# Attention 1 of a two-layer decoder: probabilities normalised on GpSimd, mask added on two blocks of three

## The reference, cut to what matters

```
x = x + L0_attn(layernorm(x)); x = x + L0_ssm(ctx, layernorm(x)); x = x + L0_ffn(layernorm(x))
x = x + L1_attn(layernorm(x)); x = x + L1_ssm(ctx, layernorm(x)); x = x + L1_moe(layernorm(x))

# L1_attn: B=4 (batches of x), S=256, H=16 query heads, 4 key/value heads, D=128
q, k = layernorm(q) * g + b, layernorm(k) * g + b          # then rotary embedding
scores  = q @ k^T / sqrt(D)                                 # 256 x 256 for each (batch, head)
scores  = where(causal, -inf, scores)
weights = softmax(scores)                                   # exp(s - max) / sum
attn    = weights @ v
out     = concat(attn over heads) @ w_o^T
```

## Time and profile before

| what | us |
|---|---|
| median of 3 runs (lowest, highest) | 913.45 (911.21, 914.03) |
| the profiled execution | 913.75 |
| its span, from the first to the last instruction | 912.0 |
| TensorE busy, over the span | 767.7 (84%) |
| VectorE busy | 703.3 (77%) |
| ScalarE busy | 445.6 (49%) |
| GpSimd busy | 340.6 (37%) |
| chain that ended last: TensorE, VectorE, issue, ScalarE, GpSimd | 50%, 26%, 11%, 9%, 3% |

### The profile page before, as it was taken

How to read it: one execution, slowest core, us unless ns; L and a number is a source line. 1 busy time by engine, 2 the same in 40 slices (tenths; PEclk the granted TensorE clock), 3 DMA queues, 4 the chain that set the end, 5 groups by cost and what they waited for, 6 DMA issues and landing times.

```text
span 912.0 us, 12288 instructions
## 1 busy us (share of the span) xinstructions
PE 767.7 (84%) x3984; PEld 563.1 (62%) x3984; DVE 703.3 (77%) x1229; ACT 445.6 (49%) x928; POOL 340.6 (37%) x242
## 2 busy tenths in 40 slices
PE   6771459877798996799999999999955799999997
PEld 2241346554433563477767776777743689999996
DVE  4869779889857976999999999999977544444443
ACT  1663368650336402666566556756642354444442
POOL 1001346552330422233333323432343286666663
PEclk9785579998799998999999999999987899999999
DMA  4313223345020212011111211111300243334431
GB/s 171 121 47 114 93 94 125 115 139 218 1 98 0 74 43 92 19 40 44 51 36 36 69 36 36 55 39 36 118 0 1 79 158 138 138 138 138 141 135 46
DMA packets 28884, 74.63 MB, mean 82 GB/s; under 512 B 3633, under 2 KB 6337, under 8 KB 28449
## 3 DMA queue, kind: packets, MB, share of 16 engines
q1 hardware_dynamic: 28384, 71.51, 23.2%
q10 hardware_dynamic: 448, 2.49, 0.8%
HBM read 72.55 MB, written 1.44 MB: 81 GB/s over the span
## 4 chain that ended last, share of the span: by engine, by line
PE 50%; DVE 26%; issue 11%; ACT 9%; POOL 3%; DMA 1%; POOLq 0%; DVEq 0%; SPq 0%; ACTq 0%
PE ps L1671 6%; PE ps L1785 6%; PE ps L1786 6%; PE ps L1787 6%; PE ps L1631 4%; DVE hS L976 3%; PE ps L1651 3%; PE ps L1750 3%; PE ps L1435 2%; PE ps L1738 2%; DVE arena L1280 2%; DVE hS L1006 2%; DVE ps L968 2%; PE ps L1408 1%; PE ps L1720 1%
## 5 line engine op out<-in xcount | busy, mean ns | idle before, releaser
L403 POOL TENSOR_TENSOR hS<-hS,BCb 128x512 f32<-128x512 f32 x64 | 81.6, 1278 | 131.9 <-issue 66.7
L1387 DVE SCALAR_TENSOR_TENSOR arena<-ps,arena 128x1024 f32<-128x1024 f32 x32 | 39.2, 1224 | 102.2 <-ACT arena L842 93.1
L426 POOL TENSOR_TENSOR hS<-hS,BCb 128x1024 f32<-128x1024 f32 x23 | 56.1, 2440 | 111.3 <-DVE ps L968 96.3
L1671 PE MATMUL ps<-WB,hT 128*128 128x512 f32 x192 | 88.0, 603 | 3.0 <-DVE arena L1261 2.0
L476 POOL TENSOR_TENSOR MHl<-arena,MHh 128x1024 fp32r<-128x1024 f32 x34 | 81.7, 2404 | 16.9 <-ACT MHh L845 16.9
L1416 PE MATMUL ps<-ident,hS 128*128 128x128 f32 x256 | 40.1, 311 | 54.7 <-POOL hS L426 31.2
L1785 PE MATMUL ps<-Wh,MHh 128*128 128x256 f32 x272 | 77.8, 286 | 6.0 <-POOL MHl L476 6.0
L1006 DVE TENSOR_TENSOR_SCAN hS<-dA,ps 128x512 f32<-128x512 f32 x64 | 78.1, 1220 | 2.2
L1786 PE MATMUL ps<-Wl,MHh 128*128 128x256 f32 x272 | 77.6, 285 | 0.0
L1787 PE MATMUL ps<-Wh,MHl 128*128 128x256 f32 x272 | 77.5, 285 | 0.0
L1416 PEld LDWEIGHTS ps<-ident,hS 128*128 128x128 f32 x256 | 32.6, 159 | 65.1 <-POOL hS L426 38.2
(11 more groups left out here) (233 smaller groups left out, 1967.4 us busy)
## 6 DMA issues: line engine op xcount, KB each, us to landing
BCb<-bc_dram SPq DMA_DIRECT2D x32, 512.0 KB, 3.7
BCb<-bcq_dram SPq DMA_DIRECT2D x64, 256.0 KB, 3.1
arena<-gate_dram SPq DMA_DIRECT2D x32, 512.0 KB, 3.7
WB<-in_we SPq DMA_DIRECT2D x34, 256.0 KB, 2.7
WB<-in_wqkv SPq DMA_DIRECT2D x1, 3072.0 KB, 12.7
WA<-in_wo ACTq DMA_DIRECT2D x1, 2048.0 KB, 7.7
WA<-in_ffn SPq DMA_DIRECT2D x1, 1408.0 KB, 7.9
pkb<-in_pk SPq DMA_DIRECT2D x2, 698.0 KB, 4.7
```

The source lines that it names most:

```text
L403: gp.tensor_tensor(h, h, qbc(q)[:, 1:2, :].broadcast_to([P, DT, S]), ALU.mult).then_inc(s["c_ready"], 1)
L426: gp.tensor_tensor(h, h, BCb[g % SB_LOADS][:, 1:2, :].broadcast_to([P, DT, HALF]), ALU.mult).then_inc(s["c_ready"], 1)
L1671: last = mm(ps[:, bank + t, :], hT[:, c, P * (2 * b + t):P * (2 * b + t) + P], WB[:, c, c0:c0 + 512], start=(c == 0), stop=(c == HC - 1))
```

## The change

Two edits, both in attention 1.

The two multiplications by the reciprocal move from VectorE to GpSimd. VectorE keeps the reciprocal, under the entry "norm" of the plan, and GpSimd takes the same entry for the multiplications. The reciprocal of unit u now also waits until GpSimd has finished unit u - 2, whose reciprocals lie in the same buffer; TensorE's transposes wait for the same semaphore as before, which GpSimd now raises.

The mask matmul writes and reads blocks 0 and 2 of the three only, 256 columns for 384. The middle block is not written by it any more; L1720's second half is the first to write there.

```diff
@@ GpSimd
+            def norm1(u):
+                p = u % 2
+                pool.wait_ge(s["s1_rc"], u + 1)
+                gp.tensor_scalar(P1[p][:, 0:P], P1[p][:, 0:P], rc1[:, p, 0:1], None, ALU.mult).then_inc(s["s1_norm"], 1)
+                gp.tensor_scalar(P1[p][:, P:3 * P], P1[p][:, P:3 * P], rc1[:, p, 1:2], None, ALU.mult).then_inc(s["s1_norm"], 1)
+
             for kind, a in ATT1_PLAN:
                 if kind == "sum":
                     job(JOB[a])
+                elif kind == "norm":
+                    norm1(a)
                 elif kind == "dbu" and a > Q_IN_FFN:
                     times_cq(a - 1)
@@ VectorE
-            def norm1(u):
+            def rc1_calc(u):
                 p = u % 2
                 dve.wait_ge(s["s1_exp"], 2 * (u + 1))
+                if u >= 2:
+                    dve.wait_ge(s["s1_norm"], 2 * (u - 1))
                 v.reciprocal(rc1[:, p, :], sum1[:, p, :]).then_inc(s["s1_rc"], 1)
-                dve.wait_ge(s["s1_rc"], u + 1)
-                v.tensor_scalar(P1[p][:, 0:P], P1[p][:, 0:P], rc1[:, p, 0:1], None, ALU.mult).then_inc(s["s1_norm"], 1)
-                v.tensor_scalar(P1[p][:, P:3 * P], P1[p][:, P:3 * P], rc1[:, p, 1:2], None, ALU.mult).then_inc(s["s1_norm"], 1)
...
                 elif kind == "norm":
-                    norm1(a)
+                    rc1_calc(a)
@@ TensorE
-                mm(ps[:, 2 + p, 0:3 * P], identb[:], mask1[:], start=True, stop=True, skip_group_check=True)
+                diagonal = lambda z: z.rearrange("p (k n) -> p k n", k=3)[:, 0::2, :]
+                mm(diagonal(ps[:, 2 + p, 0:3 * P]), identb[:], diagonal(mask1[:]), start=True, stop=True, skip_group_check=True)
```

## The result

The kernel after the change has a median of 922.12 us (921.12 to 922.98); the kernel before, measured beside it, 913.55. The ratio is 1.0099, 95% interval 1.0078 to 1.0119: **slower, by 8.6 us** (7 to 11 by the interval). I had predicted 913.0, practically no change, with a range of 909 to 922.5.

The account below looks back on a forecast made before the run. Two nearly tied loops, TensorE with ScalarE and VectorE's own pass, were taken to bound attention 1. From 913.75 us, -2.0 -0.4 +1.0 +0.8 gave 913.15, as median 912.85, rounded 913.0; range 909 to 922.5.

Parts of the forecast that it names:

- What bounds the kernel: Attention 1's three-slot pattern: a TensorE and ScalarE loop of 14.03 us nearly tied with VectorE's pass, mean 14.06.
- Rival 3: Attention 1 bound by VectorE, as its 96% busy says: 18 us faster, 895; chance 0.06.
- rival 4: Mask matmul over two separate blocks as slow as before: +1.3 us on the forecast, counted within the forecast's chance of 0.38.
- VectorE is relieved: Attention 1: 33 us of VectorE's work go, but only 0.5 us at each of four waits counts: -2.0 us.
- the long waits: Four waits of ScalarE's exponential for VectorE's maximum in attention 1, 3.1 us together, 0.5 us to be saved at each.
- The mask: Mask matmul on TensorE 0.05 us shorter: transposing slot 14.03 to 13.98, and -0.4 us outside the pattern.
- GpSimd gets 128 instructions: Price of the two moved multiplications on GpSimd: 0.85 us a pair, between a memset's 0.48 and a two-input product's 1.27.
- What the norm stands behind: Transposing slot: multiplications queue behind GpSimd's job L459 and L460, making transposes L1729 0.75 us late; period 14.05.
- the room of 0.68: Lateness of transposes L1729 that costs nothing, since TensorE's L1738 waits for ScalarE anyway: 0.68 us.
- What stands behind the norm: GpSimd's times_cq (L403), moved later, blocks VectorE's add L1274 in the rope; pattern 14.12, +1.0 us.
- Rival 1: Blocking between GpSimd and VectorE's eight rope multiplications closes a ring of 14.62 us a pattern: 921; chance 0.38.
- The end: End of attention 1: the last multiplications delay the last times_cq and TensorE's last accumulation and transposes, +0.8 us.

Follow-up runs that it names:

- e4: The kernel before with the multiplications by the reciprocal left out on both engines, so the output is not normalised; 910.92 us, ratio 0.9959.
- e6: The kernel before with the two-block mask matmul and ScalarE's copy of the transposes ahead of the scan's exponentials; 913.27 us, ratio 0.9992.
- e10: e4 with ScalarE's copy of the transposes also moved ahead of the scan's exponentials; 907.65 us, ratio 0.9933 to the kernel before.
- e1: The kernel before with the two-block mask matmul alone, multiplications still on VectorE; 914.07 us, ratio 1.0004.
- e3: The change with GpSimd's job (L459, L460) put behind the next unit's multiplications instead of ahead of them; 915.40 us, ratio 1.0024 to the kernel before.
- e5: The change with GpSimd's two multiplications as two-input products, the reciprocal broadcast as second tensor; 912.84 us, ratio 0.9984 to the kernel before.
- e8: The change with the 256-column multiplication back on VectorE and the 128-column one left on GpSimd; 913.35 us, ratio 0.9991 to the kernel before.

## Why the prediction was wrong

*What bounds the kernel: right.* Two nearly tied loops, 14.03 through TensorE and ScalarE and 14.11 through VectorE. e4 shows the first by taking the second away, e6 the second by shortening the first, and e10 shortens both. Rival 3, VectorE as the bound at 895, is refuted by e4, and rival 4 by the mask matmul's 0.11 us.

*VectorE is relieved, -2.0:* the size came out in e4 (2.0 us of the stretch), in part by luck: 0.8 of it lies in the patterns and not at the long waits, while slots 53 to 63 are 2.2 shorter and the end 1.0 longer. The change did not collect it. Slots 53 to 63 came out 0.2 shorter, since there the multiplications, now on GpSimd behind one times_cq after another, are late in place of the maxima.

*The mask, -0.4:* -0.4 in e1's stretch, and nothing in its time. I had let the transposing slot fall to 13.98 without asking what VectorE's 14.11 would then do in a kernel without the move; with VectorE relieved the 13.98 did come (e3, e5).

*GpSimd gets 128 instructions, 0.85 us the pair: this is the step that failed.* The pair took 0.61 and 0.92, together 1.5 us (1.47 from start to start), above my upper bound of 1.27. The bound was the time of a two-input product over 512 columns, taken as more than a multiplication by a per-row scalar over 384 can need. The assumption behind it, that an instruction with fewer inputs costs no more per column, is what fell: as products the same pair takes 0.93 (e5), and lies inside the bounds.

*What the norm stands behind: the mechanism right, its size wrong with the pair.* The multiplications begin where L460 ends, L1729 (L1737 after) is the one that waits, and there is a room below which lateness costs nothing (0.43 late in e5, pattern 13.98). The pair holds GpSimd for 1.47 (500.80 to 502.27). With that for 0.85 my own formula gives 1.37 late, less the room of 0.68, on 13.98: 14.67. Measured are 14.56; the 0.11 between them is L460, 1.67 here and 1.78 in the earlier trace rows. e5 tests the same formula at 0.93: 0.83 late, less 0.68, 14.13, and its L460 is 0.14 shorter: 13.99; measured 13.98. Had I put 1.47 into the sum, the pattern would have given 17 times 0.61, or +10.4, the end +1.4, and with -2.0 and -0.4 it is +9.4, or 923.2 for the profiled execution, which took 921.94. That these lie so close is partly luck: the patterns gave +6.7 and not +10.4, slots 53 to 63, with three of the four long waits, gave -0.2 and not nearly -2.0, and the end gave +2.0.

*What stands behind the norm, +1.0:* it did not bind. The add did get stretched, to 2.28 where I said some 1.9. But VectorE idles 0.37 us before L1265 and 0.49 before L1304, so no ring that closes through its rope and scan sets the period. The one that does uses VectorE from the rotation to the reciprocal alone.

*Rival 1 came close to the time for the wrong reason.* It gave 921, and patterns over 14.5 with TensorE waiting at L1729 were its signs. But its ring grows with the pair twice: at 1.47 it would be 14.62 plus twice 0.62, or 15.9, and the eight L1280 should have taken over 2.6. They took 2.33, and VectorE waited for others. e3 shows it from the other side: with the job moved behind the pair, the group of eight grew to 3.41, more than the rival had it (2.19 and 0.85), and the pattern fell to 13.98.

By the Trainium skill, "SBUF — State Buffer", section Who interferes with whom, read strictly, both multiplications should have held up the rope by their own length. The trace agrees for instructions with two inputs (L403 and the add here; L403 and the eight in e3) and disagrees for the multiplication by a per-row scalar: L466 and the end of L465 beside the eight L1288 cost them 0.14 together. As products (e5) the pair cost the eight 0.38 (2.57 for 2.19), of the 0.88 us that it ran beside them, so the blocking is partial there too. The stretched L1296 of the earlier trace rows, which the prediction named as agreeing, has one tensor input and a per-row scalar, so it is no case of the rule for two inputs.

*The end, +0.8:* +2.0. I had started the last pair at the reciprocal; it stands behind a times_cq that is itself behind the pair before, and is 0.62 longer by its price. Not all of it belongs to the pair: e4, without multiplications, has 9.4 for 8.4 there, behind slots 53 to 63 that are 2.2 shorter. From slot 53 to X together e4 took 1.2 us less than the kernel before, the change 1.8 more. I also counted 17 patterns where 15 came out as such.

## What to carry to other kernels

A bound from another kind of instruction is only a bound if the kinds are comparable: when a move's price rests on an operation that the trace does not show, let the range reach past the nearest row, and try a second form of the same operation. Before work is moved to an idle engine, look at what it will stand behind in that engine's queue at the one moment that somebody waits for it; here the same work at the same price cost 8.6 us behind a job of 1.9 us, and 1.8 us ahead of it. Where two loops are nearly tied, price an edit against the second loop, and look for the pair of edits that moves both: relief (in its cheap form and in the right place of the queue) and reordering together gave 0.7%, where the reordering alone gave nothing measurable and the relief alone, as first made, a loss.

## What the runs showed of the hardware

- On GpSimd a multiplication by a per-row scalar took, in the median, 0.61 us for 128 columns and 0.92 for 256, in place in SBUF; the same multiplication as a product with the scalar broadcast as a second tensor took 0.40 and 0.61.
- Beside VectorE's add over 1024 columns with two SBUF inputs, the scalar form was held up as well (L465 1.57 us instead of 0.61, so that it ended 0.47 after the add, which was through at 504.62), though it hardly held up the short ones: the longest L1288 in the change is 0.49, while L403 in e3 stopped one L1299 for 0.9 (1.245 instead of 0.34):

```profile
L1288 DVE SCALAR_TENSOR_TENSOR arena<-arena,jst,tabs x160: 337/343/488, 344.2 to 640.0; 128x128 f32<-128x128 f32 x160
```

```profile
L1299 DVE SCALAR_TENSOR_TENSOR arena<-arena,jst,tabs x160: 335/341/1245, 344.7 to 632.1; 128x128 f32<-128x128 f32 x160
```

- VectorE's multiplication by a per-row scalar, 256 columns in SBUF, took 1.08 us instead of 0.35 where GpSimd's L403 had started before it (e8).
- The bf16 mask matmul over two blocks that are not adjacent held TensorE for 0.11 us, two thirds of the 0.16 for three blocks: the gap in the addresses cost nothing that shows.
